# A 4-bit feed-forward stage: its steps spread over four engines, with one more slot of depth

## The reference

```
def fp4_quant_dequant(x):
    scale = max(abs(block of 16)) / 6, at least 1e-12
    idx = searchsorted([.25,.75,1.25,1.75,2.5,3.5,5.], abs(x / scale))
    return [0,.5,1,1.5,2,3,4,6][idx] * sign(x) * scale

gate = fp4(x) @ fp4(w_gate).T          # 128 -> 352
y    = fp4(x) @ fp4(w_up).T            # 128 -> 352
h    = silu(gate) * y                  # the middle values
out  = fp4(h) @ fp4(w_down).T          # 352 -> 128
x    = x + 0.5 * out
```

## Time and profile before

| | us |
|---|---|
| median of three runs | 4579.53 |
| lowest and highest | 4579.15, 4584.91 |
| span of the profiled execution | 4582.6 |
| TensorE busy in it | 3971.2 (87%) |
| VectorE busy | 3493.0 (76%) |
| ScalarE busy | 3069.3 (67%) |
| GpSimd busy | 1526.0 (33%) |

### The profile page before, as it was taken

The page is one execution under the profiler, slowest core; times in us unless marked ns, Lnnn a source line. Parts: engine busy times, 40 slices in busy tenths (PEclk is TensorE's granted clock), DMA queues, the critical chain, the costliest instruction groups (busy, mean ns, idle before and its releaser), DMA issues.

```text
span 4582.6 us, 66148 instructions
## 1 busy us (share of the span) xinstructions
PE 3971.2 (87%) x15980; PEld 2219.1 (48%) x15980; DVE 3493.0 (76%) x11277; ACT 3069.3 (67%) x5649; POOL 1526.0 (33%) x2846
## 2 busy tenths in 40 slices
PE   5688759999999999999999999994878549999965
PEld 4466624444444444444444444442555437777744
DVE  5898479888888788887887887885656956666678
ACT  3455338999899899998998998992222216666632
POOL 2322124444444444444443443443000014333310
PEclk8888769999999999999999999996999769999977
DMA  2122010000000000100000000000000001111100
GB/s 56 29 34 37 15 23 1 1 24 1 15 10 1 20 6 1 25 1 15 10 1 20 6 1 22 3 1 0 1 0 0 1 14 43 43 43 43 43 1 18
DMA packets 151432, 71.88 MB, mean 16 GB/s; under 512 B 109433, under 2 KB 141902, under 8 KB 151012
## 3 DMA queue, kind: packets, MB, share of 16 engines
q1 hardware_dynamic: 144612, 64.16, 5.6%
q10 hardware_dynamic: 6400, 3.15, 0.2%
HBM read 54.48 MB, written 12.80 MB: 15 GB/s over the span
## 4 chain that ended last, share of the span: by engine, by line
PE 55%; DVE 21%; ACT 12%; issue 8%; DMA 1%; POOL 1%; DVEq 0%; ACTq 0%; SPq 0%; POOLq 0%
PE bank L1877 19%; PE bank L1892 6%; PE bank L1921 5%; PE bank L2663 5%; PE bank L1931 3%; DVE arena L1324 2%; PE bank L2696 2%; DVE arena L1328 2%; PE bank L655 2%; ACT arena L1969 2%; ACT arena L1968 2%; ACT L2015 2%; ACT arena L1981 2%; ACT arena L1972 2%; PE bank L2723 1%
## 5 line engine op out<-in xcount | busy, mean ns | idle before, releaser
L1877 PE MATMUL bank<-arena 128*128 128x512 f32 x3072 | 1423.2, 596 | 12.6 <-DVE arena L2058 6.1
L1877 PEld LDWEIGHTS bank<-arena 128*128 128x128 f32 x3072 | 587.2, 191 | 758.7 <-issue 730.1
L2118 POOL TENSOR_SCALAR arena<-arena 128x256 f32<-128x256 f32 x1024 | 483.7, 483 | 1191.0 <-DVE arena L2051 1191.0
L1892 PE MATMUL bank<-arena 128*128 128x512 f32 x1024 | 526.6, 606 | 64.8 <-DVE arena L2081 64.4
L2040 DVE SCALAR_TENSOR_TENSOR arena<-arena 128x256 f32<-128x256 f32 x1024 | 393.9, 421 | 185.9 <-ACT arena L1969 178.1
L2081 DVE SCALAR_TENSOR_TENSOR arena<-arena 128x256 f32<-128x256 f32 x1024 | 493.5, 526 | 13.5 <-issue 12.4
L2058 DVE SCALAR_TENSOR_TENSOR arena<-bank,bv,arena 128x256 f32<-128x256 f32 x1024 | 445.1, 472 | 0.0
L1968 ACT ACTIVATE arena<-bank,bqk 128x512 f32<-128x512 f32 x512 | 348.3, 680 | 81.5 <-PE bank L1877 72.9
L2051 DVE SCALAR_TENSOR_TENSOR arena<-bank,bq,arena 128x512 f32<-128x512 f32 x512 | 384.3, 751 | 18.0
L1981 ACT ACTIVATE arena<-arena,const_table 128x512 f32<-128x512 f32 x512 | 374.5, 731 | 0.0
L1972 ACT ACTIVATE arena<-bank,bqk 128x512 f32<-128x512 f32 x512 | 354.1, 692 | 0.7 <-PE bank L1877 0.6
(11 more groups left out here) (370 smaller groups left out, 7497.0 us busy)
## 6 DMA issues: line engine op xcount, KB each, us to landing
arena<-packed_dram SPq DMA_DIRECT2D x96, 96.0 KB
arena<-packed_dram SPq DMA_DIRECT2D x32, 288.0 KB
arena<-diag_dram SPq DMA_DIRECT2D x16, 256.0 KB, 4.0
arena<-in_L_attn_Wk_dram SPq DMA_DIRECT2D x16, 256.0 KB, 3.3
arena<-in_L_attn_Wq_dram SPq DMA_DIRECT2D x16, 256.0 KB, 4.0
arena<-in_L_attn_Wv_dram SPq DMA_DIRECT2D x16, 256.0 KB, 4.5
arena<-in_L_attn_Wo_dram SPq DMA_DIRECT2D x8, 512.0 KB, 3.9
arena<-in_L_attn_W_dram SPq DMA_DIRECT2D x16, 256.0 KB, 2.8
```

Of the source, the lines that this page charges most:

```text
L1877: nc.tensor.matmul(bank[:, RING1[m % 5], :], w1p[k][:, i * P:(i + 1) * P], zT_of(g), start=True, stop=True).then_inc(a1_proj.sem, 1)
L1892: nc.tensor.matmul(bank[:, 6, :], wo1[:, i, :], a1_att[:, i % 4, :], start=(i == 0), stop=(i == NB1 - 1)).then_inc(a1_outd.sem, 1)
L2118: last = nc.gpsimd.tensor_scalar(a, a, 1.0, a1_ksum[:, i % 4, b:b + 1], ALU.add, ALU.mult)
```

## The change

- The LayerNorm apply moves from VectorE to ScalarE: one Identity with scale and bias for each tile. The bias, minus mean times rstd, is made by two new steps on GpSimd (`bias_pool`).
- The product of Silu and up values moves from VectorE to GpSimd (`h_product_pool`), one instruction over 1408 values.
- In the rounding, mask and constant are replaced by one Abs on ScalarE that writes 2^22 |v| as bfloat16 (`x_abs_act`, `h_abs_act`); add and subtract become `scalar_tensor_tensor` with a `max` against a constant. VectorE's ten steps become eight, and the scale is kept negative.
- VectorE's order in a slot: maximum of the middle values of group s-3, statistics of group s, division of s-3, all steps ahead of the Abs for input s-1, the rounding of the middle values s-3, the rounding of input s-1, add of s-4, scale of s-3. Middle values are rounded one slot later than before.
- TensorE: the down matmuls' turns are cut into three parts that stand between the two halves of `up_pe`.
- ScalarE's order: copy of the input, two copies of turned values, the four Silu and copies, the third copy, Abs of middle values, Abs of input, apply.

```diff
+            def apply_act(g, u):
+                f3_bias.wait(nc.scalar, g + rep * G)
+                xt_psum.wait_free(nc.scalar, g + n * G)
+                for q in range(QT):
+                    last = nc.scalar.activation(xn[:, u, q, :], tile(g, q), ACT.Identity,
+                                                bias=f3_nb[:, u, q:q + 1], scale=rstd[:, u, q:q + 1])
...
+            def h_product_pool(g, u):
+                s = g + rep * G
+                f3_act.wait(nc.gpsimd, s)
+                f3_hstep.wait(nc.gpsimd, s - 2, 5)
+                nc.gpsimd.tensor_tensor(f3_h[:, u, :], f3_silu[:, u, :, :].rearrange("p q f -> p (q f)"),
+                                        f3_upc[:, u, :, :].rearrange("p q f -> p (q f)"), ALU.mult)\
+                    .then_inc(f3_mul.sem, 1)
...
+            def h_abs_act(g, u):
+                f3_hstep.wait(nc.scalar, g + rep * G, 5)
+                nc.scalar.activation(f3_hm[:], f3_hv[:], ACT.Abs, scale=STEP_MAGIC).then_inc(f3_habs.sem, 1)
+
+            def h_round_dve(g, u):
+                s = g + rep * G
+                f3_habs.wait(nc.vector, s)
+                nc.vector.scalar_tensor_tensor(f3_hv[:], f3_hm[:], STEP_LEAST, f3_hv[:], ALU.max, ALU.add)\
+                    .then_inc(f3_hstep.sem, 1)
+                f3_hstep.wait(nc.vector, s, 6)
+                nc.vector.scalar_tensor_tensor(f3_hv[:], f3_hm[:], STEP_LEAST, f3_hv[:], ALU.max, ALU.subtract)\
+                    .then_inc(f3_hstep.sem, 1)
...
             programs["vector"].append(lambda e: over_groups(
-                e, [(0, stats_dve), (1, apply_dve), (1, quant_x_dve), (2, quant_h_dve), (3, add_dve)]))
-            programs["gpsimd"].append(lambda e: over_groups(e, [(0, rstd_pool)]))
+                e, [(3, h_max_dve), (0, stats_dve), (3, h_norm_dve), (1, x_norm_dve), (3, h_round_dve),
+                    (1, x_round_dve), (4, add_dve), (3, h_scale_dve)]))
+            programs["gpsimd"].append(lambda e: over_groups(e, [(0, rstd_pool), (0, bias_pool), (2, h_product_pool)]))
             programs["tensor"].append(lambda e: over_groups(
-                e, [(0, transpose_pe), (0, up_pe), (1, down_pe)], gate(e, n)))
+                e, [(0, transpose_pe), (0, up_pe((0, 1))), (2, turn_pe(0)), (2, turn_pe(1)), (0, up_pe((2, 3))),
+                    (2, turn_pe(2)), (2, down_pe)], gate(e, n)))
             programs["scalar"].append(lambda e: over_groups(
-                e, [(0, copy_act), (0, silu_act), (1, copy_h_act)], gate(e, n)))
+                e, [(2, copy_act), (4, copy_h_act(0)), (4, copy_h_act(1)), (2, silu_act), (4, copy_h_act(2)),
+                    (3, h_abs_act), (1, x_abs_act), (0, apply_act)]))
```

More of the change, by code:

```diff
@@ L779, in ffn3, with bias_pool @@
         def ffn3(n, rep):
-            stats_dve, rstd_pool, apply_dve, _, copy_act = ln_steps(n, 1e-5)
-            def quant_x_dve(g, u):
+            stats_dve, rstd_pool, _, _, copy_act = ln_steps(n, 1e-5)
+            by_block = lambda a: a.rearrange("p (n k) -> p n k", k=BLOCK)
+            spread = lambda a, nb: a.unsqueeze(2).to_broadcast([P, nb, BLOCK])
+            def bias_pool(g, u):
                 s = g + rep * G
-                ln_applied.wait(nc.vector, g + n * G)
[L786 to L792, removed]
+                ln_rstd.wait(nc.gpsimd, g + n * G)
+                nc.gpsimd.tensor_tensor(f3_nb[:, u, :], meanvar[:, u, :, 0], rstd[:, u, :], ALU.mult)\
+                    .then_inc(f3_bias.sem, 1)
+                f3_bias.wait(nc.gpsimd, s, 1)
+                apart(nc.gpsimd)
+                nc.gpsimd.tensor_scalar(f3_nb[:, u, :], f3_nb[:, u, :], -1.0, None, ALU.mult).then_inc(f3_bias.sem, 1)
@@ new lines, in x_abs_act, with x_round_dve @@
+            def x_abs_act(g, u):
+                f3_xstep.wait(nc.scalar, g + rep * G, 5)
+                nc.scalar.activation(f3_xm[:], f3_xv[:], ACT.Abs, scale=STEP_MAGIC).then_inc(f3_xabs.sem, 1)
+            def x_round_dve(g, u):
+                s = g + rep * G
+                f3_xabs.wait(nc.vector, s)
+                nc.vector.scalar_tensor_tensor(f3_xv[:], f3_xm[:], STEP_LEAST, f3_xv[:], ALU.max, ALU.add)\
+                    .then_inc(f3_xstep.sem, 1)
+                f3_xstep.wait(nc.vector, s, 6)
+                nc.vector.scalar_tensor_tensor(f3_xv[:], f3_xm[:], STEP_LEAST, f3_xv[:], ALU.max, ALU.subtract)\
+                    .then_inc(f3_xstep.sem, 1)
+                f3_xstep.wait(nc.vector, s, 7)
+                nc.vector.tensor_tensor(by_block(f3_xq[:, u, :, :].rearrange("p q d -> p (q d)")),
+                                        by_block(f3_xv[:]), spread(f3_xs[:], NBX), ALU.mult)\
+                    .then_inc(f3_xstep.sem, 1)
@@ L799, in transpose_pe, with up_pe, fn @@
                 last.then_inc(xt_psum.sem, 1)
[L801 to L810, removed]
+            def up_pe(qs):
+                def fn(g, u):
+                    s = g + rep * G
+                    xt_ready.wait(nc.tensor, g + n * G)
+                    if n and isinstance(g, int) and g == 0:
+                        x_written.wait(nc.tensor, n * G - 1)
+                    for q in qs:
+                        f3_act.wait_free(nc.tensor, s, q + 1)
+                        nc.tensor.matmul(bank[:, 2 + 2 * (q % 2), 0:FF3], xT_tile(u, q), wgT[:], start=True, stop=True)
+                        nc.tensor.matmul(bank[:, 3 + 2 * (q % 2), 0:FF3], xT_tile(u, q), wuT[:], start=True, stop=True)\
+                            .then_inc(f3_up.sem, 1)
+                return fn
             def silu_act(g, u):
@@ L827, in quant_h_dve, with h_max_dve @@
                     .then_inc(f3_mul.sem, 1)
+            def h_max_dve(g, u):
+                s = g + rep * G
                 f3_mul.wait(nc.vector, s)
-                f3_turned.wait_free(nc.vector, s)
[L830 to L841, removed]
+                nc.vector.tensor_reduce(f3_hs[:, u, :], by_block(f3_h[:, u, :]), AX.X, ALU.max, apply_absolute_value=True)\
+                    .then_inc(f3_hstep.sem, 1)
+                f3_hstep.wait(nc.vector, s, 1)
+                nc.vector.tensor_scalar(f3_hs[:, u, :], f3_hs[:, u, :], -1.0 / 6.0, -1e-12, ALU.mult, ALU.min)\
+                    .then_inc(f3_hstep.sem, 1)
@@ new lines, in h_scale_dve, with turn_pe, fn @@
+            def h_scale_dve(g, u):
+                s = g + rep * G
+                f3_turned.wait_free(nc.vector, s)
+                f3_hstep.wait(nc.vector, s, 7)
+                nc.vector.tensor_tensor(by_block(f3_hq[:, u, :, :].rearrange("p q f -> p (q f)")),
+                                        by_block(f3_hv[:]), spread(f3_hs[:, u, :], NBH), ALU.mult)\
+                    .then_inc(f3_hstep.sem, 1)
+            def turn_pe(i):
+                r0, rows = F3B[i]
+                def fn(g, u):
+                    s = g + rep * G
+                    f3_hstep.wait(nc.tensor, s)
@@ L848, in down_pe, with copy_h_act, fn @@
                     last.then_inc(f3_turned.sem, 1)
+                return fn
+            def copy_h_act(i):
+                r0, rows = F3B[i]
+                def fn(g, u):
+                    s = g + rep * G
+                    if i == 0:
+                        f3_psum.wait_free(nc.scalar, s)
+                    f3_turned.wait(nc.scalar, s, i + 1)
+                    nc.scalar.activation(f3_hT[0:rows, u, i, :], bank[0:rows, 6 + i % 2, :], ACT.Copy)\
+                        .then_inc(f3_copied.sem, 1)
+                return fn
+            def down_pe(g, u):
+                s = g + rep * G
                 f3_copied.wait(nc.tensor, s)
```

70 lines of the change are left out of this document (50 added, 20 removed).

## The result

The changed kernel takes 4591.46 us (median of 11 runs, 4586.49 to 4595.79) where the kernel before takes 4579.13 (11 runs beside it, 4572.19 to 4584.91): ratio 1.0029, 95% interval 1.0021 to 1.0036, slower by 0.2 to 0.4%. The forecast was 4599.

A forecast was written before the change was run, and what follows sets the result against it. VectorE's chain bounds the old slot at 21.97 us; afterwards a TensorE-ScalarE round trip of 21.3 does. 45.7 + 6 x 21.3 + 0.2 + 11.75 + 0.15 = 185.6 a stage, 19.6 longer for both: 4599 us, range 4552 to 4636.

The forecast's parts named there:

- The ring: In ffn3, the round trip through TensorE and ScalarE between input roundings replaces VectorE as the bound: 21.3 us a slot.
- 1 to 3: TensorE after the input's rounding: transpose with ScalarE's copy, up_pe for two tiles, two turns of group g-2; end at 7.5 us.
- 4: ScalarE, in order: copy of part 1, Silu and copy of tile 0, then the bank is free for up_pe: 1.65 us.
- 5: Two more tiles 2.4, last Silu and copy 0.95, copy of part 2, Abs 1.37, a hop 0.15 us.
- 6: VectorE's rounding passes: two of 1408 values, 3.3 us, and three of 512, 2.2 us.
- the block: GpSimd's product holds up VectorE's first pass over 1408 values: between 0 and 1.25 us a slot, 1.25 taken.
- two table loads a slot: Rival: Abs not in Silu's table set, so loads before Abs and Silu; round trip 2.6 us longer, 4641 us; chance 0.04.
- clock stays up: Rival: TensorE's gaps don't lower its clock; round trip 17.5 to 18.8 us, 4560 us taken; chance 0.26.
- Lower level throughout: Rival: TensorE at its lower clock for the whole round trip, 24.85 us with the block, 4641 us; chance 0.12.
- no block: Rival: GpSimd's product does not hold VectorE, clock as assumed; round trip 20.05 us, 4575 us; chance 0.16.
- the stage's sum: First statistics to last turn of an ffn3 stage: 185.6 us against 175.8, so 9.8 us longer each stage.
- the last rival: Abs not in the table set with Silu, two table loads in each slot, 4641 us; chance 0.04.

The follow-up runs named there:

- e8: The changed kernel with five unused 128x512 matmuls behind each group's down matmuls and one of 320 columns between transpose and gate matmuls: 4564.10 us.
- e7: The changed kernel with GpSimd multiplying only one tile of four (352 of 1408 columns), the rest of the product left out: 4568.43 us.
- e4: The changed kernel with ScalarE's Abs of the middle values moved between the second and third Silu: 4573.35 us.
- e6: The kernel before with one part of the change alone, the LayerNorm apply on ScalarE and its bias on GpSimd: 4569.03 us.
- e11: The changed kernel with Abs between second and third Silu, product on VectorE, and VectorE's scale ahead of the residual add: 4531.23 us.
- e2: The changed kernel with the LayerNorm apply back on VectorE and without the two bias steps on GpSimd: 4584.63 us.
- e10: The changed kernel with Abs between second and third Silu, product on VectorE, and eight unused 128x512 matmuls ahead of the down matmuls: 4582.94 us.
- e1: The changed kernel with the product of Silu and up values back on VectorE, ahead of the block maximum: 4573.62 us.
- e5: The changed kernel with the Abs of the middle values between second and third Silu and the product back on VectorE: 4545.16 us.
- e3: The changed kernel with four unused 128x512 matmuls of constants behind each group's down matmuls: 4590.47 us.

## Why the prediction came out as it did

**The ring was right.** The prediction's steps, read off the slot above from the end of the rounding at 3642.37 (3641.68 + 0.69) to the next one's end at 3663.20:

| step | forecast | measured |
|---|---|---|
| 1 to 3: transpose, copy, two tiles, two turns | 7.5 | 7.34 (turns end 3648.67 + 1.04) |
| 4: ScalarE frees the bank | 1.65 | 1.45 |
| 5: two tiles, Silu, copy, Abs | 5.4 | 5.26 (to 3656.42) |
| 6: passes, with the block | 6.75 | 6.78 |
| sum | 21.3 | 20.83 |

In stage 2 the slots settle at 20.45. Three slips in the prediction's working change nothing here: the terms of the lower level add up to 23.4, not 23.6; two table loads a slot (2.6 us) would give some 4630, not 4641; and the middle of "clock stays up" (-11 and -35 us) is 4556, not 4552. The Abs over 1408 took 1.38 (1.37 forecast), the product 3.18 (3.3).

**The clock: the level was right, the moment of the rise was partly luck.** I took the rise 6.3 us after the rounding from "the middle" of eight restarts, given as 6.5. The range, 2.8 to 9.3 us, is right, but the clock in windows of the profile, 0.5 us each, behind the eight turns of stage 1 in before gives 2.8, 3.4, 7.7, 8.4, 8.9, 9.0, 9.3 and 9.3: their middle is 8.6. With that, steps 1 to 3 would have been at the lower level to their end, 1.95 + 4.7 + 1.9 = 8.55 us instead of 7.5, and the forecast some 12 us higher. In after the same windows put the rise 7.7, 6.4, 5.7, 5.4 and 5.2 us after the rounding in stage 1, from the third input on, and 4.8 to 5.1 in stage 2. From one rounding to the next it is 21.8, 21.2, 20.8, 20.65 and 20.5 us, and 20.4 to 20.5 in stage 2: the slots differ by half of what the rise is late, as they should where matmuls of 352 columns start 1.17 us apart at the lower level and 0.59 at the upper, so this one term accounts for their whole spread. In the slot above the rise is at 3648.1, and the first gate matmul began 2.01 us after the rounding (1.95 forecast for the lower level). "Clock stays up" did not come true, the clock was 0.77 over the stage; e8, which forces it, gives 4564 where that rival was put at 4560. "Lower level throughout" did not either.

**The block.** I took 1.25 us a slot from a row of another stage, between 0 and 1.25. It is 1.45 in this slot: the product runs until 3658.00, 1.58 us into the pass, and the pass ends 1.49 behind that. Once the nearest row was believed, the price was the rest of the product at the pass's start, which I had at 1.3. Where no product runs beside it, the pass has its own length, as in the last group of after:

```profile
3730.80 1.62 DVE L916 SCALAR_TENSOR_TENSOR arena<-arena 128x1408 f32<-128x1408 bf16 x1 [1.44 <-ACT arena L911]
```

e7 measures what the "no block" rival claimed: 4568, forecast for it 4575. The Trainium skill (SBUF — State Buffer, "Who interferes with whom") says that whoever issues first holds the shared ports for a whole instruction and that the order decides who blocks; the pairs of e4, 4.60 against 1.62 and 4.58 against 3.18, agree with it in both directions. The power of the earlier trace rows that left VectorE alone does not, and no run here explains it.

**What failed was a size: the stage's sum.** 9.8 us more a stage were forecast, 4.3 and 0.9 came. In stage 1 the rounding of the third input ends at 3599.39, 44.1 us after the first statistics, not 45.7. Here the block shows in the fill too: the first product starts at 21.17 (21.3 forecast) and holds the second input's rounding.

```profile
3576.79 3.33 DVE L840 SCALAR_TENSOR_TENSOR arena<-arena 128x512 f32<-128x512 bf16 x1 [7.71 <-ACT arena L835]
```

The pass takes 3.33 instead of 0.69 and ends 0.54 us behind the product (3580.12 against 3579.58). The product itself ends at 24.3, where the sum has 24.8, and the rounding is done at 26.3 instead of 27.0, and the next one 17.8 us later instead of 18.7. Five round trips took 105.0 instead of 106.5. The tail, from the last input's rounding (3704.38) to the last add's end (3745.15), took 40.8; the prediction has 185.6 - 45.7 - 106.5 = 33.4 to the last turn, and behind it the 9.8 of before, 43.2. Of the 2.4 between, 0.7 lie ahead of the last pass but one (3718.20), 0.5 in the last group, and 0.9 behind the last turn, where TensorE still began at the upper level (clock 1.00 from 3736.0 to 3736.5, 0.50 from 3737.0 on), behind 2.39 us of idle time instead of 4.59, and rose to it again near 3743.7, before the down matmuls ended (12 transposes in 2.55 us, 2.92 in the earlier trace rows; down matmuls in 4.91, 5.49 in before):

```profile
3736.27 2.55 PE L940 MATMUL bank<-const_table,arena 128*128 128x128 f32 x12 [2.39 <-DVE arena L926]
```

1.6 + 1.5 + 2.4 = 5.5 us less than the sum; 9.8 - 5.5 = 4.3. Stage 2 of after is 2.6 us shorter than its stage 1, with its rises sooner after the rounding, and before's stage 2 is 0.8 longer: 0.9.

**The time still came within 8 us of the forecast, and that was in part luck.** The stages account for 5.2 us of the 12, where 19.6 were forecast; the rest is nothing that the prediction has. In the pair of profiles 6.2 us stand ahead of the first `ffn3` stage (its first statistics at 3549.03 and 3555.25). The same code stands there in every kernel of the table, and in their profiled executions these statistics begin between 3540.6 (e6) and 3556.1 (e11); the rest of an execution takes 4200 to 4218 us, 4211 in before. So the 5 to 7 us can't be put down to the change from one pair of executions. One thing does separate the kernels: at the same LayerNorm step (L310), which starts 525 us into before, the eleven kernels made from after are 2.9 to 10.7 us later than before, and e6, made from before, 0.1 earlier. A loss early in the program that comes with the changed program is thus suggested, and not explained. One part has a row, in unchanged code of the first attention stage. Before, then after (GpSimd clears memory, VectorE applies the LayerNorm to four tiles):

```profile
65.39 7.65 POOL L1704 MEMSET arena<- 128x2048 f32 x7
65.48 5.53 DVE L326 TENSOR_SCALAR xn<-x,meanvar,rstd 128x128 f32<-128x128 f32 x4 [1.52 <-POOL rstd L319]
```

```profile
65.55 7.37 POOL L1809 MEMSET arena<- 128x2048 f32 x7
65.64 7.93 DVE L326 TENSOR_SCALAR xn<-x,meanvar,rstd 128x128 f32<-128x128 f32 x4 [1.51 <-POOL rstd L319]
```

Four such instructions take 1.12 us otherwise. Here, beside the seven clears, their time differs: 5.53 us in before, e2 and e10, 6.42 in e6, 7.93 in after and eight others. That is 2.4 us of the 6.2 in this pair. The cause of the rest stays open; no run here separates what the edit does to it from chance.

**The table loads** stand once a stage, before the first Silu, and none before an Abs, so the last rival is out. ScalarE's groups in the first stage of after have this one:

```profile
L877 ACT ACT_TABLE_LOAD x1 | 1.3, 1283 | 2.9 <-PE bank L866 2.9
```

**One term of the first part was wrong and did not matter.** I put VectorE's own work at 16.4 us a slot. e11, where VectorE alone sets the period, takes 16.87 with the product's 1.65 in it, so 15.2 without: the small gaps between dependent steps went too, since other steps now stand between them. With the ring at 20.45 that made the hole longer, nothing else.

## What to carry to other kernels

- Where one engine is full, taking work from it pays only until the round trip through the others is longer than its queue. Write that round trip down step by step, with the queue position of each short step: the Abs of 1.38 us cost more by standing behind four Silus than by its length (e1 to e5, which differ in that alone: slots of 18.55 to 20.0 us, then 17.6). e5 and e11 keep the change's split of the work and only put two steps elsewhere in their queues and the product back, and turn +12 us into -51.
- An elementwise product on GpSimd beside VectorE steps with two inputs is not free time. Each such pair pays the rest of whichever began first, 1.45 us in the slot of after and about 3 in those of e4, and moving the Abs ahead in its queue (e4) moved the payment to other instructions.
- The edit that is worth 1.3 us a slot in the kernel where VectorE is full (e6) is worth nothing a slot in the one where it has a hole (e2).

## What the runs showed of the hardware that I had not expected

- The block reaches GpSimd's smallest steps. The bias product over 4 elements takes 0.20 us alone and 0.96 beside VectorE's pass over 1408 (after, GpSimd's timeline):

```profile
3558.20 0.20 POOL L801 TENSOR_TENSOR f_nb<-meanvar,rstd 128x4 f32<-128x4 f32 x1
...
3649.26 0.96 POOL L801 TENSOR_TENSOR f_nb<-meanvar,rstd 128x4 f32<-128x4 f32 x1
```

- Beside seven memory clears on GpSimd four of VectorE's one-input `tensor_scalar` took 5.53 to 7.93 us instead of 1.12, with the same code. That the clears hold them is not shown: no experiment was made on it.
- Unused matmuls shorten this kernel by 27 us (e8) when they fill both gaps of a slot, and not measurably (e3, 1 us) when they leave 1.8 and 0.8 us of the two open. A matmul of 512 columns on 32-bit data costs 0.88 us (7.03 / 8).
